# Two graph layers with residual norm: x kept on chip, turned blocks in the banks of row sums, a fourth bank for second products

## The chip, the cores and the metric

The kernel runs on one core of one Trainium2 chip. The metric is the device time of one execution in microseconds (us), lower is better. TensorE multiplies into PSUM, which has eight banks; VectorE, ScalarE and GpSimd work on SBUF and PSUM; SyncE (SP) issues the DMAs, all into one queue that sixteen DMA engines serve.

## The reference

```python
def reference(x, adj, u, weight, bias):          # x 8192x64, adj 8192x8192, f32
    keep = (u >= 0.1)
    h = layernorm(x + adj @ (x * keep / 0.9))
    return layernorm(h + adj @ (h @ weight) + bias)
```

adj is 256 MB of f32. Both layers multiply with all of it, and the second needs h, which needs the first.

## The kernel before

adj is cut into 16 x 16 tiles of 512 x 512, 1 MB each (four parts of 128 rows of the contraction). Tile (i, j) serves row i (output rows) and takes column block j. SBUF has 17 slots for tiles. `order_of_work` writes out a fixed list of jobs before the program is built, and `place_tiles` gives each tile a slot. TensorE works off the list in order. SP issues the loads in the same order, and each waits until the job that freed its slot is done (`tile_jobs_done`). The 256 tiles take 334 MB of loads: the list is made so that most tiles serve both layers with one load, and the rest come twice.

The kinds of jobs that matter here:
- `part`: row 0, in four parts. `part_turn` turns a part's block.
- `first` (L986): a tile's share of x's product, into the bank of row sums `sum_f[i % 2]`, of which it uses the left half.
- `second` (L1039), `pair` (L1033, two tiles), `both`, `early` (L1019), `chunk` and `rest` (L953, L954): products with h or with both operands. Each takes a bank out of `echo`, in turn, and VectorE adds it into its home in SBUF (L654 in the profile, called by `join`) and counts `added`. TensorE may not write a bank again before it was added.
- `raw` and `fused`: one tile for both layers with fewer multiplications; VectorE makes sums of the tile for them, and `combine` puts the products together at the end of the row.

When a row's sums are complete (`row_end`), VectorE copies them together with the shares from SBUF into `halves` (L841, L843), transposes them into the bank `turned` (L762), adds x (L776, eight instructions), and normalises (`normalise`, to L736). The result h is written to `stat`, beside the masked x that the first layer's matmuls use: `stat[:, block, 0:64]` holds masked x, `stat[:, block, 64:128]` is empty until h is there. Behind each row's end TensorE has a filler of some six halves of a job before it needs that h. x itself is loaded row by row into `x_res` (L486), two rows deep. At the start x and u come together in four loads `xu` into the last four slots, where VectorE makes masked x of them (L633).

The eight banks of PSUM: two for `products`, two for `sum_f`, one for `turned`, three for `echo`.

Of the kernel before, what the change touches and what calls it, by code (L numbers as in the profile page):

```python
# [27 lines left out]
ACT = mybir.ActivationFunctionType  # L28
# [19 lines left out]
FILL = 6  # L48
ECHO_BANKS = 3
WORK = {"chunk": 11, "rest": 11, "first": 11, "second": 11, "both": 22, "fused": 19, "pair": 22, "early": 44}  # L50
# [56 lines left out]
def turns(i):  # L107

    return i + PARTS
# [30 lines left out]
def order_of_work():  # L140
# [35 lines left out]
    for i in range(1, NB):  # L176
# [6 lines left out]
        while sum(HALVES[job[0]] for job in filler) < FILL:  # L183
            choice = [early] if lead < LEAD and early else [again] if i > 7 else []
            choice = [jobs_of for jobs_of in (*choice, light, again, early, heavy, near) if jobs_of]
            if pieces and (len(filler) == ECHO_BANKS if i > 1 else len(filler) % 2 == 0):
                filler += pieces.pop(0)
            else:
                filler.append(choice[0].pop(0))
            for job in filler[taken:]:  # L190
                put(job)
            taken = len(filler)
            if not turned:
                turned = True
                if i == 1:
                    jobs.append(("part_turn", PARTS - 1))
# [99 lines left out]

def resnorm_graph_layers(nc: bass.Bass, x, xu, adj_t, adj_parts, adj_0, adj_chunks, weight, bias, out):
    jobs = order_of_work()
# [37 lines left out]

    x_v = x.rearrange("(b p c) d -> p b (c d)", p=P, c=C)
    out_v = out.rearrange("(b p c) d -> p b (c d)", p=P, c=C)

    ctx = ExitStack()  # L340
    with ctx:
        def sb(name, shape):
            return ctx.enter_context(nc.sbuf_tensor(name, shape, F32))

        def sem(name):
# [9 lines left out]
        third = sb("third_partial", [P, B // 2])  # L355
        x_res = sb("x_res", [P, 2, C * D])
        halves = sb("halves", [P, B])
# [9 lines left out]

        h_bias = [x_res[:, :, :].rearrange("p n (c d) -> p (n c) d", d=D),
                  halves[:, :].rearrange("p (c d) -> p c d", d=D)]
        w2 = sb("w2", [P, 2 * D])  # L370
# [28 lines left out]
        def layer2_block(i):  # L399
# [5 lines left out]
            "p s (b n k d) -> p s b n k d", b=PARTS, n=2, d=D)  # L405

        psum = ctx.enter_context(nc.psum_tensor("psum", [P, 8, B], F32))
        banks = [psum[:, n] for n in range(8)]
        products = banks[0:2]
        sum_f = banks[2:4]  # L410
        turned = banks[4]
        echo = banks[5:8]
        scale_sum = echo[ECHO_BANKS - 1][:, 0:1]
# [20 lines left out]
        s_xu = [sem(f"xu_loaded_{n}") for n in range(XU)]  # L434
        s_res = [sem(f"x_res_loaded_{n}") for n in range(2)]
        s_small = sem("weight_bias_loaded")
        s_out = sem("out_stored")
        tile_jobs_done = sem("tile_jobs_done")
        dropped = sem("x_dropped")
        zeroed = sem("sums_zeroed")  # L440
        identity = sem("identity_ready")
# [29 lines left out]
        @block.sync  # L471
        def _(sp):
            for g in range(XU):
                sp.dma_start(tiles[:, staged + g], xu[g]).then_inc(s_xu[g], 16)
            rows_begun = 0
            for n, (tile, part, slot, freed, new, kind) in enumerate(loads):
                if n == len(loads) // 2:
                    for at in (0, D):
                        for beside in (0, D):
                            sp.dma_start(w2[at:at + D, beside:beside + D], weight).then_inc(s_small, 16)  # L480
                    sp.dma_start(bias_b[:, :], bias.rearrange("(a d) -> a d", a=1).to_broadcast([P, D])).then_inc(s_small, 16)
                if rows_begun == 0 and part == 1 or rows_begun >= 1 and kind in ("first", "fused") and tile[0] == rows_begun:
                    i = rows_begun
                    if i >= 2:
                        sp.wait_ge(turned_read, turns(i - 2))
                    sp.dma_start(x_res[:, i % 2], x_v[:, i]).then_inc(s_res[i % 2], 16)  # L486
                    rows_begun += 1
                if new and staged <= slot:
                    sp.wait_ge(dropped, XU)
                if freed:  # L490
                    sp.wait_ge(tile_jobs_done, freed)
                if part is not None:
                    to, source = tiles[:, slot, part], adj_parts[part, tile[1]]
                elif kind == "part":
                    to, source = tiles[:, slot], adj_0[tile[1], tile[2] - 1]
                elif kind == "chunk":
                    to, source = tiles[:, slot], adj_chunks[tile[1], tile[2]]
                else:
                    to, source = tiles[:, slot], adj_t[tile]
                sp.dma_start(to, source).then_inc(s_part[part] if part else s_arrived[slot], 16)  # L500
            for n, i in (*enumerate(finals[:-2]), (len(finals) - 1, finals[-1]), (len(finals) - 2, finals[-2])):
                if n == len(finals) - 1:
                    sp.wait_ge(last_y_ready, 1)
                else:
                    sp.wait_ge(y_ready, n + 1)
                sp.dma_start(out_v[:, i:i + 2], layer2[:, i // 2].rearrange("p (b k) -> p b k", b=2)).then_inc(s_out, 16)
            sp.wait_ge(s_out, 16 * len(finals))
# [31 lines left out]
        def _(act):  # L539
            norms = 0  # L540

            def norm(squares, centred_rows, root_ap, var_ap):
# [5 lines left out]
                act.activation(root_ap, var_ap, ACT.Sqrt).then_inc(rooted, 1)  # L548

            for job in jobs:  # L550
                if job[0] == "part_end":
# [23 lines left out]
        def _(dve):  # L575
# [54 lines left out]
            for g in range(XU):  # L630
                dve.wait_ge(s_xu[g], 16)
                t = slice(g * PARTS * C, (g + 1) * PARTS * C)
                dve.scalar_tensor_tensor(  # L633
                    out=stat[:, t, 0:D].rearrange("p (b k) d -> p b k d", b=PARTS), in0=xu_stage[:, g, :, 1], scalar=DROP,
                    in1=xu_stage[:, g, :, 0], op0=ALU.is_ge, op1=ALU.mult).then_inc(dropped, 1)
                dve.wait_ge(dropped, g + 1)
                dve.tensor_reduce(out=largest[:, g:g + 1], in_=stat[:, t, 0:D], axis=AX.XY,
                                  op=ALU.max).then_inc(dve_step, 1)
# [100 lines left out]
            def turn_part(q):  # L739

                rows = r[:, q:q + 1, :]
                t = turned[:, :].rearrange("p (c f) -> p c f", c=C)[:, q:q + 1]
                dve.wait_ge(s_res[0], 16)
                if q:
                    dve.wait_ge(h_ready, q)
                dve.wait_ge(turned_ready, q + 1)
                step(dve.scalar_tensor_tensor(out=rows, in0=t[:, :, 0:D], scalar=KEPT,
                                              in1=x_res[:, 0].rearrange("p (c d) -> p c d", c=C)[:, q:q + 1],
                                              op0=ALU.mult, op1=ALU.add))
# [5 lines left out]
            def turn(i):  # L755


                k = turns(i) - 1
                dve.wait_ge(s_res[i % 2], 16 * (i // 2 + 1))
                dve.wait_ge(h_ready, k)  # L760
                source = sum_f[i % 2] if i < EARLY else halves
                last = dve.transpose(turned[:, 0:B // 2], source[:, 0:B // 2])  # L762
                if i < EARLY:
                    last.then_inc(half_by_dve, 1)
                    dve.wait_ge(half_by_dve, turns(i))
                else:
                    step(last)
                t = turned[:, 0:B // 2].rearrange("p (c e f) -> p c e f", c=C, f=QUAD)
                x_rows = x_res[:, i % 2].rearrange("p (c d) -> p c d", c=C)
                for side in range(2):  # L770
# [104 lines left out]
        def _(pe):  # L875
# [29 lines left out]
            for at, job in enumerate(jobs):  # L905
                kind = job[0]
                if kind == "part":
                    _, q, g = job
                    bank = part_bank(q)
                    if g == 0 and q >= 2:  # L910
                        pe.wait_ge(half_by_act, q - 1)
                        pe.wait_ge(half_by_dve, q - 1)
                    if g == 0 and q:
# [20 lines left out]
                elif kind == "part_turn":  # L934
# [6 lines left out]
                    pe.wait_ge(half_by_dve, q + 1)  # L941
                    pe.transpose(turned[:, of_part(q)], halves[:, of_part(q)], ident[:, :]).then_inc(turned_ready, 1)
                elif kind in ("chunk", "rest"):
# [12 lines left out]
                elif kind in ("raw", "fused", "first", "both"):  # L956
# [21 lines left out]
                    elif kind != "fused":  # L978
                        if begun.get("f") != i:
                            if i <= 2:  # L980
                                pe.wait_ge(half_by_act, turns(i - 2))
                            pe.wait_ge(half_by_dve, turns(i - 2))
                        ends = jobs[at + 1] == ("row_end", i)
# [64 lines left out]
                elif kind == "final":  # L1048
# [3 lines left out]
                    if n_final >= 2:  # L1052
                        pe.wait_ge(product_read, n_final - 1)
                    else:
                        pe.wait_ge(half_by_dve, turns(NB - 1))
                        pe.wait_ge(combined, 2 * combined_rows(NB - 1))
# [45 lines left out]
```

## Time and profile before

| | |
|---|---|
| median of 3 runs | 898.15 us (898.11 to 898.16) |
| profiled execution | 898.45 us, span 896.5 us |
| TensorE busy | 863.1 us (96%), mean granted clock 0.995 |
| VectorE busy | 560.9 us (63%) |
| ScalarE, GpSimd busy | 21.3 us, 25.3 us |
| main DMA queue | 358.74 MB, 96.9% of sixteen engines' span |
| x loads | 16 of 128 KB |

Busy shares are means over the whole span. The time of an execution is somewhat longer than the span, which runs from the first to the last instruction. Matmuls come as two records each, and two of them run side by side, so the time of a group is read from its first start to the next group's start.

### The profile page before, as it was taken

How to read it: one execution, taken by the hardware profiler on the slowest of the kernel's cores; microseconds unless marked ns; L12 is line 12 of the kernel's file. 1: busy time of each engine (PE TensorE's matmuls, PEld its weight loads, DVE VectorE, ACT ScalarE, POOL GpSimd, SP SyncE). 2: the span in 40 equal slices, each digit the busy share in tenths (PEclk: the TensorE clock that was granted, in tenths of full speed). 3: DMA queues.
4: the chain of work that ended last, by engine and by line, in shares of the span. 5: the costliest groups of instructions: out<-in, count | busy, mean ns of one | idle time of the engine just before them, and what ended most of it. 6: DMA issues, size and time to landing. Idle time of an engine off the chain costs nothing.

```text
span 896.5 us, 15757 instructions
## 1 busy us (share of the span) xinstructions
PE 863.1 (96%) x6790; PEld 482.7 (54%) x6790; DVE 560.9 (63%) x1144; ACT 21.3 (2%) x59; POOL 25.3 (3%) x24
## 2 busy tenths in 40 slices
PE   3899999999999999999999999999999999999996
PEld 2664554445767546555555564646545566456432
DVE  6356123145155757775777777778777777867755
ACT  0100000000000000000000000000000000000011
POOL 3000000000000000000000000000000000000133
PEclk9999999999999999999999999999999999999998
DMA  9999999999999999999999999999999999999962
GB/s 373 412 416 420 421 419 420 421 420 421 420 420 420 419 421 419 421 400 402 420 421 406 423 419 397 419 372 422 372 410 421 415 423 419 420 423 419 420 256 71
DMA packets 55412, 359.73 MB, mean 401 GB/s; under 512 B 6448, under 2 KB 10544, under 8 KB 12592
## 3 DMA queue, kind: packets, MB, share of 16 engines
q1 hardware_dynamic: 55344, 358.74, 96.9%
q8 instruction: 54, 0.88, 0.4%
q14 instruction: 14, 0.11, 0.0%
HBM read 356.61 MB, written 2.10 MB: 400 GB/s over the span
## 4 chain that ended last, share of the span: by engine, by line
PE 85%; DMA 7%; DVE 4%; SPq 2%; issue 2%; ACT 0%; POOLq 0%; POOL 0%; DVEq 0%
PE psum L1033 20%; PE psum L986 19%; PE psum L967 8%; PE psum L1001 8%; PE psum L995 8%; PE psum L1019 6%; DMA tiles<-adj_chunks 5%; PE psum L953 5%; PE psum L974 4%; PE psum L1039 4%; DMA tiles<-adj_t 2%; PE psum L930 1%; SPq L500 1%; DVE layer L654 1%; DVE layer L709 1%
## 5 line engine op out<-in xcount | busy, mean ns | idle before, releaser
L986 PE MATMUL psum<-tiles,stat 128*64 128x256 f32 x1952 | 218.3, 379 | 1.6 <-DMA tiles<-adj_t 1.6
L1033 PE MATMUL psum<-tiles,stat 128*64 128x512 f32 x944 | 210.3, 593 | 0.6 <-issue 0.3
L654 DVE TENSOR_TENSOR layer<-psum,layer 128x512 f32<-128x512 f32 (+1 forms) x143 | 98.7, 690 | 154.6 <-PE psum L1033 58.0
L986 PEld LDWEIGHTS psum<-tiles,stat 128*64 128x64 f32 x1952 | 147.1, 137 | 72.4 <-issue 7.5
L1033 PEld LDWEIGHTS psum<-tiles,stat 128*64 128x64 f32 x944 | 69.2, 137 | 119.8 <-issue 115.8
L690 DVE TENSOR_TENSOR tiles<-tiles 128x512 f32<-128x512 f32 x90 | 62.2, 691 | 53.8 <-PE psum L976 52.2
L1003 PE MATMUL psum<-tiles,stat 128*64 128x256 f32 x360 | 92.6, 380 | 0.0
L969 PE MATMUL psum<-tiles,stat 128*64 128x256 f32 x360 | 92.4, 379 | 0.0
L967 PE MATMUL psum<-tiles,stat 128*64 128x256 f32 x360 | 92.4, 379 | 0.0
L967 PEld LDWEIGHTS psum<-tiles,stat 128*64 128x64 f32 x360 | 49.3, 137 | 37.8 <-issue 16.7
L678 DVE TENSOR_TENSOR tiles<-tiles 128x512 f32<-128x512 f32 x90 | 60.6, 684 | 8.0 <-DMA tiles<-adj_t 8.0
L693 DVE TENSOR_TENSOR tiles<-tiles 128x512 f32<-128x512 f32 x90 | 62.3, 692 | 3.1
L695 DVE TENSOR_TENSOR tiles<-tiles 128x512 f32<-128x512 f32 x90 | 61.6, 684 | 0.0
L1019 PE MATMUL psum<-tiles,stat 128*64 128x512 f32 x256 | 56.3, 593 | 2.9 <-issue 2.9
L930 PE MATMUL psum<-tiles,stat 128*64 128x128 f32 x512 | 34.1, 292 | 17.4 <-DMA tiles<-adj_parts 15.6
L969 PEld LDWEIGHTS psum<-tiles,stat 128*64 128x64 f32 x360 | 49.3, 137 | 0.0
L1001 PE MATMUL psum<-tiles,stat_homes 128*64 128x256 f32 x192 | 49.3, 379 | 0.0
L995 PE MATMUL psum<-tiles,stat_homes 128*64 128x256 f32 x192 | 49.3, 379 | 0.0
L997 PE MATMUL psum<-tiles,stat_homes 128*64 128x256 f32 x192 | 49.3, 379 | 0.0
L1003 PEld LDWEIGHTS psum<-tiles,stat 128*64 128x64 f32 x360 | 48.8, 137 | 0.0
L953 PE MATMUL psum<-tiles,stat 128*64 128x512 f32 x96 | 45.1, 600 | 0.9 <-DMA tiles<-adj_chunks 0.9
L954 PE MATMUL psum<-tiles,stat 128*64 128x512 f32 x96 | 45.1, 600 | 0.0
(100 smaller groups left out, 852.5 us busy)
## 6 DMA issues: line engine op xcount, KB each, us to landing
tiles<-adj_t SPq DMA_DIRECT2D x306, 1024.0 KB, 13.6
tiles<-adj SPq DMA_DIRECT2D x12, 1024.0 KB, 19.2
tiles<-adj_chunks SPq DMA_DIRECT2D x12, 1024.0 KB, 20.4
tiles<-xu SPq DMA_DIRECT2D x4, 1024.0 KB, 8.0
tiles<-adj_parts SPq DMA_DIRECT2D x16, 256.0 KB, 17.6
x_res<-x SPq DMA_DIRECT2D x16, 128.0 KB, 14.4
out<-layer SPq DMA_DIRECT2D x8, 256.0 KB, 2.2
w<-weight SPq DMA_DIRECT2D x4, 16.0 KB, 10.2
```

The source lines that it names most:

```text
L654: return dve.tensor_tensor(out=to, in0=addend, in1=to, op=ALU.add)
L690: dve.tensor_tensor(out=tile[:, top, left], in0=tile[:, top, left], in1=tile[:, top, right], op=ALU.add).then_inc(operands_ready, 1)
L693: dve.tensor_tensor(out=tile[:, bottom, left], in0=tile[:, bottom, left], in1=tile[:, top, left], op=ALU.add).then_inc(operands_ready, 1)
L953: pe.matmul(bank[0:D, :], stat[:, c, half], moving[:, n], start=True, stop=True)
L967: pe.matmul(products[0][low, left], stat[:, j * C + k, 0:D], tile[:, k, left], start=new and k == 0, stop=False, skip_group_check=True)
L969: pe.matmul(products[0][high, left], stat[:, j * C + 2 + k, 0:D], tile[:, 2 + k, left], start=new and k == 0, stop=False, skip_group_check ...
L986: last = pe.matmul(sum_f[i % 2][to, left], stat[:, j * C + c, 0:D], tile[:, c, columns], start=begun.get("f") != i and c == 0, stop=ends a ...
L995: pe.matmul(products[1][low, left], t[:, 2, k], tile[:, k, left], start=False, stop=False, skip_group_check=True)
L1001: pe.matmul(products[0][low, right], t[:, 1, k], tile[:, 2 + k, right], start=False, stop=False, skip_group_check=True)
L1003: last = pe.matmul(products[0][high, right], stat[:, j * C + 2 + k, D:2 * D], tile[:, 2 + k, left], start=False, stop=False, skip_group_ch ...
L1019: last = pe.matmul(bank[to, :], stat[:, j * C + c, half], tile[:, c], start=c == 0, stop=c == C - 1)
L1033: last = pe.matmul(bank[to, :], stat[:, j * C + c, D:2 * D], tile[:, c], start=c == 0, stop=c == C - 1)
```

## The change

- While `xu` lies in its slots, ScalarE copies x out of it into the half of `stat` where h will stand (`x_kept` counts the copies). VectorE reads x from there when it turns a row, and h is written over it afterwards. The loads into `x_res`, their semaphores and the DRAM argument `x` go. SP waits for `x_kept` before it loads into the slots of `xu`.
- `turned` has no bank of its own any more: a turned block goes to the right half of the bank of row sums that it comes from. TensorE therefore waits for `turned_read` (the turned block was read) where it waited for the copies of the sums.
- The bank that comes free is a fourth one for `echo`.
- In `order_of_work` the number of light jobs ahead of the pieces in a row's filler was `ECHO_BANKS`, 3; it is now a constant of its own, 2.
- `h_bias` at the end of the kernel uses two free blocks of `layer1`.

```diff
-ECHO_BANKS = 3
+ECHO_BANKS = 4
+JOINS_LAST = 2
...
-            if pieces and (len(filler) == ECHO_BANKS if i > 1 else len(filler) % 2 == 0):
+            if pieces and (len(filler) == JOINS_LAST if i > 1 else len(filler) % 2 == 0):
...
-        x_res = sb("x_res", [P, 2, C * D])
...
-        h_bias = [x_res[:, :, :].rearrange("p n (c d) -> p (n c) d", d=D),
-                  halves[:, :].rearrange("p (c d) -> p c d", d=D)]
+        h_bias = [layer1[:, n].rearrange("p (c d) -> p c d", d=D) for n in (1, 2)]
...
+        def rows_of_x(g, half):
+
+            return stat[:, g * PARTS * C:(g + 1) * PARTS * C, half].rearrange("p (b k) d -> p b k d", b=PARTS)
...
-        turned = banks[4]
-        echo = banks[5:8]
+        turned = [bank[:, B // 2:B] for bank in sum_f]
+        echo = banks[4:8]
...
-                if rows_begun == 0 and part == 1 or rows_begun >= 1 and kind in ("first", "fused") and tile[0] == rows_begun:
-                    i = rows_begun
-                    if i >= 2:
-                        sp.wait_ge(turned_read, turns(i - 2))
-                    sp.dma_start(x_res[:, i % 2], x_v[:, i]).then_inc(s_res[i % 2], 16)
-                    rows_begun += 1
                 if new and staged <= slot:
                     sp.wait_ge(dropped, XU)
+                    sp.wait_ge(x_kept, XU)
...
+            for g in range(XU):
+                act.wait_ge(s_xu[g], 16)
+                act.activation(rows_of_x(g, slice(D, 2 * D)), xu_stage[:, g, :, 0], ACT.Copy).then_inc(x_kept, 1)
...
-                dve.wait_ge(s_res[i % 2], 16 * (i // 2 + 1))
                 dve.wait_ge(h_ready, k)
                 source = sum_f[i % 2] if i < EARLY else halves
-                last = dve.transpose(turned[:, 0:B // 2], source[:, 0:B // 2])
+                last = dve.transpose(turned[i % 2], source[:, 0:B // 2])
...
-                t = turned[:, 0:B // 2].rearrange("p (c e f) -> p c e f", c=C, f=QUAD)
-                x_rows = x_res[:, i % 2].rearrange("p (c d) -> p c d", c=C)
+                t = turned[i % 2].rearrange("p (c e f) -> p c e f", c=C, f=QUAD)
+                x_rows = stat[:, i * C:(i + 1) * C, D:2 * D]
...
                     if g == 0 and q >= 2:
-                        pe.wait_ge(half_by_act, q - 1)
-                        pe.wait_ge(half_by_dve, q - 1)
+                        pe.wait_ge(turned_read, q - 1)
...
                         if begun.get("f") != i:
-                            if i <= 2:
-                                pe.wait_ge(half_by_act, turns(i - 2))
-                            pe.wait_ge(half_by_dve, turns(i - 2))
+                            pe.wait_ge(turned_read, turns(i - 2))
...
                     if n_final >= 2:
                         pe.wait_ge(product_read, n_final - 1)
                     else:
-                        pe.wait_ge(half_by_dve, turns(NB - 1))
+                        pe.wait_ge(turned_read, turns(NB - 1))
                         pe.wait_ge(combined, 2 * combined_rows(NB - 1))
```

How it moves instructions. SP's queue of DMAs, where rows 1 and 2 begin; before (L500 loads a tile, L486 a row of x):

```order
L500 DMA tiles<-adj_chunks 128x2048 [waits tile_jobs_done] x2
L486 DMA x_res<-x 128x256
L500 DMA tiles<-adj_t 128x2048 [waits tile_jobs_done] x8
L500 DMA tiles<-adj_chunks 128x2048 [waits tile_jobs_done]
L500 DMA tiles<-adj_t 128x2048 [waits tile_jobs_done] x3
L500 DMA tiles<-adj_chunks 128x2048 [waits tile_jobs_done]
L500 DMA tiles<-adj_t 128x2048 [waits tile_jobs_done] x7
L486 DMA x_res<-x 128x256 [waits turned_read]
L500 DMA tiles<-adj_t 128x2048 [waits tile_jobs_done] x3
L500 DMA tiles<-adj_chunks 128x2048 [waits tile_jobs_done]
```

and now (L496 loads a tile):

```order
L496 DMA tiles<-adj_chunks 128x2048 [waits tile_jobs_done] x2
L496 DMA tiles<-adj_t 128x2048 [waits tile_jobs_done] x8
L496 DMA tiles<-adj_chunks 128x2048 [waits tile_jobs_done]
L496 DMA tiles<-adj_t 128x2048 [waits tile_jobs_done] x3
L496 DMA tiles<-adj_chunks 128x2048 [waits tile_jobs_done]
L496 DMA tiles<-adj_t 128x2048 [waits tile_jobs_done] x9
L496 DMA tiles<-adj_chunks 128x2048 [waits tile_jobs_done]
```

The x loads are gone from between the tiles; the last tile of the chunks comes one load earlier or later.

TensorE towards the end of row 2, before (L1019 are heavy jobs, L986 light ones):

```order
L1019 MATMUL psum<-tiles,stat 64x512 [waits second_added]
L1019 MATMUL psum<-tiles,stat 64x512 x7
L986 MATMUL psum<-tiles,stat 64x256 [waits tile_arrived_1]
L986 MATMUL psum<-tiles,stat 64x256 x7
L986 MATMUL psum<-tiles,stat 64x256 [waits tile_arrived_6]
L986 MATMUL psum<-tiles,stat 64x256 x7
L986 MATMUL psum<-tiles,stat 64x256 [waits tile_arrived_13]
L986 MATMUL psum<-tiles,stat 64x256 x7
L986 MATMUL psum<-tiles,stat 64x256 [waits tile_arrived_14]
L986 MATMUL psum<-tiles,stat 64x256 x7
```

and now (L1014 heavy, L981 light):

```order
L981 MATMUL psum<-tiles,stat 64x256 [waits tile_arrived_11]
L981 MATMUL psum<-tiles,stat 64x256 x7
L981 MATMUL psum<-tiles,stat 64x256 [waits tile_arrived_1]
L981 MATMUL psum<-tiles,stat 64x256 x7
L1014 MATMUL psum<-tiles,stat 64x512 [waits second_added,tile_arrived_13,tile_arrived_6]
L1014 MATMUL psum<-tiles,stat 64x512 x7
L1014 MATMUL psum<-tiles,stat 64x512 [waits second_added]
L1014 MATMUL psum<-tiles,stat 64x512 x7
L981 MATMUL psum<-tiles,stat 64x256 [waits tile_arrived_14]
L981 MATMUL psum<-tiles,stat 64x256 x7
```

One heavy job with its two tiles has moved into row 2, between the light ones, from behind the row's end.

ScalarE at the start of the program, now:

```order
L548 ACT_TABLE_LOAD
L548 ACTIVATE stat<-tiles 128x16x64 [waits xu_loaded_0]
L548 ACTIVATE stat<-tiles 128x16x64 [waits xu_loaded_1]
L548 ACTIVATE stat<-tiles 128x16x64 [waits xu_loaded_2]
L548 ACTIVATE stat<-tiles 128x16x64 [waits xu_loaded_3]
L552 ACTIVATE halves<-psum 64x128 [waits tile_jobs_done]
```

The four copies stand between the load of the table and the copy of the first part's sums; before, nothing stood there.

## Rows read from the trace of the kernel before

**Rows 1.** The page, parts 1 and 3: busy time and share, DMA queue.
```profile
PE 863.1 (96%) x6790; PEld 482.7 (54%) x6790; DVE 560.9 (63%) x1144; ACT 21.3 (2%) x59; POOL 25.3 (3%) x24
...
q1 hardware_dynamic: 55344, 358.74, 96.9%
```

**Rows 2.** Stretches of 25 us: busy time per engine, clock, DMA share, GB/s.
```profile
300.00:325.00 25.00, 23.89 (x220) 15.16 (x218) 17.13 (x44) 0.62 (x2) 0.00 (x0) 1.00 1.02 420
...
425.00:450.00 25.00, 24.69 (x196) 14.06 (x194) 17.85 (x44) 0.62 (x2) 0.00 (x0) 1.00 1.02 422
...
575.00:600.00 25.00, 25.00 (x185) 13.07 (x183) 18.94 (x47) 0.62 (x2) 0.00 (x0) 1.00 0.92 377
```

**Rows 3.** The chain that ended last: start us, us, what.
```profile
142.16 1.73 PE psum L986 x16
143.88 3.43 PE psum L1033 x16
...
305.47 18.73 DMA tiles<-adj_t
...
442.12 0.31 issue
```

**Rows 4.** Timeline of TensorE at two stalls: start, us, what, idle before.
```profile
187.07 8.37 PE L1019 MATMUL psum<-tiles,stat 128*64 128x512 f32 x38 [1.89 <-issue]
...
324.25 1.95 PE L986 MATMUL psum<-tiles,stat 128*64 128x256 f32 x16 [0.54 <-DMA tiles<-adj_t]
```

**Rows 5.** Waits from 446 us to the end: us in total, times, longest.
```profile
PE psum L1039 <- DVE layer L654: 1.4, 1, 1.4
...
PE psum L1033 <- DVE layer L654: 0.3, 1, 0.3
```

**Rows 6.** DMA issues, page part 6: count, KB each, us to landing.
```profile
x_res<-x SPq DMA_DIRECT2D x16, 128.0 KB, 14.4
```

**Rows 7.** x loads issued to 305.5 and to 424.2; DMA from 22.9 to 24.2.
```profile
L486 SPq DMA_DIRECT2D x_res<-x x7: 431/506/2073, 6.8 to 291.6; - x7
...
L486 SPq DMA_DIRECT2D x_res<-x x9: 431/432/2073, 6.8 to 380.0; - x9
...
DMA packets 289, 0.50 MB, mean 386 GB/s; under 512 B 30, under 2 KB 58, under 8 KB 289
```

**Rows 8.** Timeline of TensorE and VectorE, end of row 14.
```profile
769.95 10.47 PE L1033 MATMUL psum<-tiles,stat 128*64 128x512 f32 x48
...
772.38 0.42 DVE L841 TENSOR_TENSOR halves<-psum,layer 64x256 f32<-64x256 f32 x1
...
779.47 0.48 DVE L736 SCALAR_TENSOR_TENSOR stat<-work,h_scale,rstd 128x256 f32<-128x256 f32 x1
...
780.96 2.29 DVE L654 TENSOR_TENSOR layer<-psum,layer 128x512 f32<-128x512 f32 x3
781.80 1.94 PE L1039 MATMUL psum<-tiles,stat 128*64 128x512 f32 x8 [1.37 <-DVE layer L654]
```

**Rows 9.** Timeline of TensorE, end of row 15.
```profile
837.09 10.47 PE L1033 MATMUL psum<-tiles,stat 128*64 128x512 f32 x48
847.82 3.65 PE L1033 MATMUL psum<-tiles,stat 128*64 128x512 f32 x16 [0.26 <-DVE layer L654]
```

**Rows 10.** A ScalarE group; timeline of VectorE and SP at the start.
```profile
L546 ACT ACTIVATE work<-layer 128x512 f32<-128x512 f32 x6 | 3.8, 630 | 27.7 <-DVE layer L851 27.7
...
13.17 1.22 DVE L633 SCALAR_TENSOR_TENSOR stat<-tiles 128x1024 f32<-128x1024 f32 x1
...
28.99 2.13 SPq L500 DMA_DIRECT2D tiles<-adj_chunks  x1
```

**Rows 11.** Instructions that read x_res, by line; groups of the transposition.
```profile
L776 DVE SCALAR_TENSOR_TENSOR work<-psum,x_res x120: 279/286/297, 132.2 to 843.0; 32x128 f32<-32x128 f32 x120
...
L762 DVE STREAM_TRANSPOSE psum<-halves 128x256 f32<-128x256 f32 x14 | 6.4, 460 | 0.5
...
L762 DVE STREAM_TRANSPOSE psum<-psum 128x256 f32<-128x256 f32 x1 | 0.5, 465 | 6.2 <-PE psum L986 6.2
```

More of the change, by code:

```diff
@@ L294, in place_tiles, with resnorm_graph_layers @@
     return loads, place
-def resnorm_graph_layers(nc: bass.Bass, x, xu, adj_t, adj_parts, adj_0, adj_chunks, weight, bias, out):
+def resnorm_graph_layers(nc: bass.Bass, xu, adj_t, adj_parts, adj_0, adj_chunks, weight, bias, out):
     jobs = order_of_work()
@@ L434, in resnorm_graph_layers @@
         s_xu = [sem(f"xu_loaded_{n}") for n in range(XU)]
-        s_res = [sem(f"x_res_loaded_{n}") for n in range(2)]
         s_small = sem("weight_bias_loaded")
@@ L439, in resnorm_graph_layers @@
         dropped = sem("x_dropped")
+        x_kept = sem("x_kept")
         zeroed = sem("sums_zeroed")
@@ L474, in _ @@
                 sp.dma_start(tiles[:, staged + g], xu[g]).then_inc(s_xu[g], 16)
-            rows_begun = 0
             for n, (tile, part, slot, freed, new, kind) in enumerate(loads):
@@ L633, in _ @@
                 dve.scalar_tensor_tensor(
-                    out=stat[:, t, 0:D].rearrange("p (b k) d -> p b k d", b=PARTS), in0=xu_stage[:, g, :, 1], scalar=DROP,
+                    out=rows_of_x(g, slice(0, D)), in0=xu_stage[:, g, :, 1], scalar=DROP,
                     in1=xu_stage[:, g, :, 0], op0=ALU.is_ge, op1=ALU.mult).then_inc(dropped, 1)
@@ L741, in turn_part @@
                 rows = r[:, q:q + 1, :]
-                t = turned[:, :].rearrange("p (c f) -> p c f", c=C)[:, q:q + 1]
-                dve.wait_ge(s_res[0], 16)
+                t = turned[part_bank(q)][:, 0:P].unsqueeze(1)
+                dve.wait_ge(x_kept, XU)
                 if q:
@@ L747, in turn_part @@
                 step(dve.scalar_tensor_tensor(out=rows, in0=t[:, :, 0:D], scalar=KEPT,
-                                              in1=x_res[:, 0].rearrange("p (c d) -> p c d", c=C)[:, q:q + 1],
+                                              in1=stat[:, q:q + 1, D:2 * D],
                                               op0=ALU.mult, op1=ALU.add))
@@ L941, in _ @@
                     pe.wait_ge(half_by_dve, q + 1)
-                    pe.transpose(turned[:, of_part(q)], halves[:, of_part(q)], ident[:, :]).then_inc(turned_ready, 1)
+                    pe.transpose(turned[part_bank(q)][:, 0:P], halves[:, of_part(q)], ident[:, :]).then_inc(turned_ready, 1)
                 elif kind in ("chunk", "rest"):
@@ L1086 @@
     arrays = {
-        "x": np.ascontiguousarray(x),
         "xu": np.ascontiguousarray(xu).reshape(XU, P, C, B),
```

1 line of the change is left out of this document (removed).

## The prediction

> **What bounds the kernel now.** I read the page first for the shares. TensorE is busy for 863.1 us of 896.5, and the DMA queue fills 96.9% of sixteen engines' span [rows 1]. Two resources near their limit are an average over stages, so the next view is the table of stretches. It splits the run. At 300 to 325 us the DMA moves 420 GB/s at a share of 1.02 while TensorE has gaps, 23.89 of 25 us; at 425 to 450 TensorE has almost none at 422 GB/s; at 575 to 600 TensorE is at 25.00 and the DMA has sagged to 377 GB/s [rows 2]. So tiles set the pace first and matmuls later. The chain of work that ended last shows the change-over. It goes through a DMA only three times, and the last is a 1 MB tile issued at 305.47 us that takes 18.73 us to land, at 324.20 [rows 3]. TensorE's own line shows who waited for it: a group of 16 matmuls, 1.73 us of work [rows 3], begins at 324.25 after 0.54 us of idle put down to the tile's DMA [rows 4]. What arrives earlier before that point makes the kernel shorter. What arrives earlier behind it is worth something only where TensorE still waits for it.
>
> Behind it the list of waits from 446 us to the end has two of note for the long matmuls, and both end with VectorE's L654: 1.4 us at L1039 and 0.3 us at L1033 [rows 5]. L654 adds a bank of second products into its home and so frees the bank; TensorE had used up its three.
>
> **The x loads.** The change takes away sixteen loads of 128 KB [rows 6]. Seven of them are issued before the deciding tile is [rows 7]. They stand ahead of it in the same queue, which is never empty there, so their time is what the tile comes earlier. At the full 420 GB/s, 131,072 B take 0.31 us. In a short stretch at 23 us, where one such load lands, the mean is 386 GB/s [rows 7]; that makes 0.34 us. Seven are 2.2 to 2.4 us, and I take 2.4. TensorE can use it: the stalls of 1.89 us at 187 and 0.54 us at 324 [rows 4] and those between them are there to be given back.
>
> The next thing that could hold TensorE is at 442.12, where the chain has 0.31 us of "issue" ahead of a group of L1033 [rows 3]; the profile names nobody. If it is a tile landing, that wait shrinks too, since nine x loads have gone by then [rows 7]: plus 0.3. If not: plus 0. I take 0.3, since the DMA still runs at 422 GB/s in that stretch [rows 2]. The DMA part is 2.7 us, between 2.2 and 2.9 (nine at 0.31 are 2.8). The seven loads of x behind it count for nothing.
>
> One page of the Trainium skill would price the loads higher. "DMA: Bandwidth & Descriptors", section Bandwidth, gives 0.95 us for 64 KB by itself and 6.15 us for 1 MB; by it the seven would be worth at least 6.7 us and the kernel would take some 889 us, an estimate. The trace speaks against it: in this queue 1 MB takes 2.5 us of the stream.
>
> **The fourth bank of second products.** Row 14 first. Three pairs, 48 records of L1033, begin at 769.95 [rows 8]. At 3.43 us for 16 [rows 3] they end at 780.25, but the next group, L1039, begins at 781.80. VectorE is late: it comes to the first half of the row sums (L841) at 772.38, then has to turn and normalise, and reaches the first L654 at 780.96 [rows 8]. With four banks L1039 need not wait for that addition. It still needs h of row 14, which L736 writes from 779.47 for 0.48 us, to 779.95 [rows 8]: 0.3 us before 780.25. The gain is 781.80 - 780.25 = 1.55 us. Next late could be the pair behind it, which takes the first bank again: it would begin at 780.25 + 1.72 = 781.97, and the first addition ends at 780.96 + 0.69 = 781.65. So nothing.
>
> Row 15 has the same picture. Three pairs from 837.09 end at 847.39, and the fourth begins at 847.82 [rows 9]: 0.43 us. Together 2.0 us. Bounds: 1.7 by the idle time [rows 5], 2.0 by the starts, and 0 from below, should L1039 have to wait for h after all. Both lie behind the last tile wait, so they come on top of the DMA part. Behind 851 us TensorE goes from pair to product without a stop of note, so the last additions and stores shift with it. In the first 130 us the bank waits exist too, but tiles set the pace there: 0.
>
> **What is added.** Four ScalarE copies of 128x1024. A 128x512 takes 0.63 us [rows 10], so at most 1.3 each and 5 in all. The fourth source is there before VectorE begins its fourth pass at 13.17 [rows 10]; the copies end by 15, while ScalarE has no other work. SP's new wait stands at the load that it issues at 28.99 [rows 10]: 14 us of cover. Without that cover the queue would run dry, and each microsecond would cost one. I put 0.
>
> Waits on the copies of a block become waits on its reading. For row i TensorE asks that row i-2 has been turned. Fifteen rows are turned between 132.2 and 843.0 [rows 11], 51 us apart on average, so that is long past: 0. L776 reads x from another tensor in the same shape, 0.29 us each: 0. The transposition inside one bank is there once already, at 465 ns against 460 from SBUF [rows 11]: 0.
>
> **The moved jobs.** In rows 2 and 3 the pairs of heavy jobs (L1019) come one or two light jobs earlier, and one of them ahead of row 2's end. The work and the tiles up to row 4 are the same. TensorE work that comes sooner only moves the stall of 1.89 us at 187, and the tile that lands at 324 has the same bytes before it. Behind row 2's end two heavy jobs still stand ahead of the first use of its h, more than the chain to h needs (7.6 us in row 14, from 772.38 to 779.95). 0.
>
> **Sum.** 2.7 + 2.0 = 4.7 us. The profiled execution took 898.45 us for a span of 896.5 and so would take 893.75; it stands 0.3 above the median of 898.15, and from that: 893.4.
>
> **Rivals.**
> Only the banks help. The x loads are hidden if TensorE can't move up, for instance if VectorE holds it at 324 as well. The profile puts that wait down to the DMA alone. 898.15 - 2.0 = 896.2.
> Only the loads help. L1039 in row 14 needs h, with 0.3 us of cover; a bank wait may also only move one group on. 898.15 - 2.7 = 895.4.
> Nothing comes of either, 898.15: it would take a queue that is not the limit before 324, against 420 GB/s at a share of 1.02.
> Small loads cost more than their bytes. At twice the share of the stream, 0.68 us, the time is 898.15 - 7 x 0.68 - 0.3 - 2.0 = 891.1. The 386 GB/s speak against it. The skill's page above would have it so.
> The other side: the turned block in a bank of row sums makes VectorE's chain of each row longer. It touches that bank with the transposition and eight L776, 0.47 + 2.52 = 3.0 us a row. Cover is 0.3 us in row 14 and in a plain row 10.3 us of filler (three groups of 3.43) less 7.6, that is 2.7. If these nine took twice as long, row 14 would lose 2.7 us, six other rows behind 446 us 0.3 each, and row 14's gain of 1.55 would be gone: 898.15 - 2.7 - 0.4 + 2.7 + 1.8 = 899.6. It gets slower than before from about 2.8 us more a row. Against it: meanwhile the matmuls of the next row write the other of the two banks.
>
> **Chances.** Forecast 0.70, with a range of its own of 892.3 to 894.6; only the loads 0.11; only the banks 0.06; nothing 0.04; dearer loads 0.05; slower 0.04. The range for 8 in 10 holds the forecast and the loads-only case: 892.0 to 895.9. A change of 0.2%, 1.8 us, is about what a measurement can tell from none. Under 896.35 lie the forecast, the loads-only case, the dearer loads and most of banks-only: faster 0.90, same 0.06, slower 0.04.
>
> **What the profile after would show.** No x load among the DMA issues. The deciding tile landing near 321.8, and no matmul behind it that waits for a DMA. L1039 of row 14 straight behind its three pairs, and no wait on L654 in row 15. ScalarE's copies over by 15 us. Wrong would be: a wait ended by a tile behind 330 us, a longer L776, L1039 waiting for h, or SP held at 29 us.

## The result and the profile after

The changed kernel takes 892.86 us, median of 4 runs (892.74 to 893.27), against 898.15 us (898.11 to 898.23): a ratio of 0.9941, 95% interval 0.9929 to 0.9954. That is 5.29 us less; the forecast was 4.7 less. The profiled execution took 893.27 us for a span of 891.5 us, where before it took 898.45 us for 896.5: 5.0 us less in the span.

The page of the kernel after, parts 1 and 3, in the columns of [rows 1]:

```profile
PE 861.4 (97%) x6790; PEld 489.3 (55%) x6790; DVE 560.9 (63%) x1144; ACT 25.6 (3%) x63; POOL 25.3 (3%) x24
...
q1 hardware_dynamic: 53040, 356.64, 96.8%
```

TensorE runs the same 6790 matmuls, ScalarE four instructions more. The queue moves 358.74 - 356.64 = 2.10 MB less, the sixteen loads of 128 KB; the group of [rows 6] is gone from the DMA issues. The shares tell nothing else, so the next view is the same three stretches as in [rows 2]:

```profile
300.00:325.00 25.00, 24.04 (x217) 15.00 (x214) 16.03 (x42) 0.62 (x2) 0.00 (x0) 1.00 1.01 419
425.00:450.00 25.00, 25.00 (x188) 13.26 (x186) 18.05 (x45) 0.62 (x2) 0.00 (x0) 1.00 1.01 421
575.00:600.00 25.00, 25.00 (x172) 12.06 (x168) 17.34 (x44) 0.62 (x2) 0.00 (x0) 1.00 0.92 369
```

At 300 to 325 TensorE still has gaps and the DMA still runs at 419 GB/s: tiles still set the pace there. At 425 to 450 the 0.31 us that TensorE lacked before are back. The chain of work that ended last shows the change-over (first fence), and the timeline of TensorE shows who waited (second; start us, us, what, idle before in brackets):

```profile
303.50 18.36 DMA tiles<-adj_t
321.90 1.95 PE psum L981 x16
```

```profile
321.90 1.95 PE L981 MATMUL psum<-tiles,stat 128*64 128x256 f32 x16 [0.54 <-DMA tiles<-adj_t]
...
436.17 7.04 PE L1028 MATMUL psum<-tiles,stat 128*64 128x512 f32 x32
443.03 3.62 PE L981 MATMUL psum<-tiles,stat 128*64 128x256 f32 x32
446.49 1.89 PE L1034 MATMUL psum<-tiles,stat 128*64 128x512 f32 x8
```

The deciding tile lands at 303.50 + 18.36 = 321.86 us, before at 324.20 [rows 3]: 2.34 us sooner, and the same 0.54 us of idle stands ahead of its matmuls. It is the last DMA in the chain. At the place of the "issue" at 442.12 [rows 3] the 32 matmuls of L1028 (L1033 before) now stand in one piece. The same place in the kernel before:

```profile
438.51 3.60 PE L1033 MATMUL psum<-tiles,stat 128*64 128x512 f32 x16
442.42 3.65 PE L1033 MATMUL psum<-tiles,stat 128*64 128x512 f32 x16 [0.31 <-issue]
445.88 3.75 PE L986 MATMUL psum<-tiles,stat 128*64 128x256 f32 x32
449.46 1.89 PE L1039 MATMUL psum<-tiles,stat 128*64 128x512 f32 x8
```

From 438.51 to 449.46 it took 10.95 us, and after, from 436.17 to 446.49, 10.32 us for the same work: 0.63 us went, twice the printed 0.31. 0.48 of it lies at the gap itself (442.42 - 438.51 = 3.91 us from start to start, 3.43 without a gap [rows 3]), 0.15 in the 48 matmuls behind it. Most of that 0.15 is a second wait, which the rows of the matmuls do not print. The rows of the weight loads do, and they name the DMA; before and after:

```profile
447.68 1.49 PEld L986 LDWEIGHTS psum<-tiles,stat 128*64 128x64 f32 x16 [0.33 <-DMA tiles<-adj_t]
```

```profile
443.04 3.17 PEld L981 LDWEIGHTS psum<-tiles,stat 128*64 128x64 f32 x30 [0.28 <-issue]
```

So the last tile that TensorE waited for before was not that of 324. It is one that is issued at 430.09 and lands 17.6 us later, at 447.7, behind ten x loads; after, it lands at 444.3 and nothing waits for it.

The end of row 14 on TensorE and VectorE answers to [rows 8], the end of row 15 to [rows 9]:

```profile
766.95 10.47 PE L1028 MATMUL psum<-tiles,stat 128*64 128x512 f32 x48
777.25 1.89 PE L1034 MATMUL psum<-tiles,stat 128*64 128x512 f32 x8
```

```profile
776.46 0.48 DVE L735 SCALAR_TENSOR_TENSOR stat<-work,h_scale,rstd 128x256 f32<-128x256 f32 x1
...
777.95 2.28 DVE L653 TENSOR_TENSOR layer<-psum,layer 128x512 f32<-128x512 f32 x3
```

```profile
832.50 13.90 PE L1028 MATMUL psum<-tiles,stat 128*64 128x512 f32 x64
```

L1034 (before L1039) begins at 777.25, 10.30 us after the three pairs, as forecast, and before the first addition of L653 (before L654) at 777.95. h was there at 776.46 + 0.48 = 776.94, so the cover was 0.31 us. In row 15 four pairs stand in one piece of 64. The waits of TensorE from 446 us to the end, in the columns of [rows 5], hold neither of the two that stood there:

```profile
PE psum L1059 <- DVE layer L653: 0.3, 1, 0.3
```

(This one is a wait at a line of the last products. It stands there in every kernel of this study.) ScalarE's fourth copy, and the reading of the turned block (L774, before L776) with its transposition (L760, before L762), whose rows of before are in [rows 10, 11]:

```profile
13.39 1.06 ACT L548 ACTIVATE stat<-tiles 128x1024 f32<-128x1024 f32 x1 [1.44 <-DMA tiles<-xu]
```

```profile
L774 DVE SCALAR_TENSOR_TENSOR work<-psum,stat x120: 277/286/299, 133.3 to 838.4; 32x128 f32<-32x128 f32 x120
...
L760 DVE STREAM_TRANSPOSE psum<-halves 128x256 f32<-128x256 f32 x14 | 6.4, 460 | 0.5
```

The copies are over at 14.45 us, 9 us before SP comes to the first load that waits for them, the same load that it issued at 28.99 before [rows 10]:

```profile
23.55 7.96 SPq L496 DMA_DIRECT2D tiles<-adj_chunks  x1
```

Neither of the two that now work in a bank of row sums got longer: a median of 286 ns and a mean of 460 ns, as before.

So the time came from two places. By the starts of the same jobs, TensorE is ahead by 324.25 - 321.90 = 2.35 us at the deciding tile, by 449.46 - 446.49 = 2.97 at 446 us, and in row 14 by 781.80 - 777.25 = 4.55. Row 15 adds its share (847.82 less the start of the fourth pair, 832.50 + 10.30 = 842.80, is 5.02), and at that the spans' 5.0 us are full.

One more thing belongs to these numbers. The profiled execution after is the longest of its four, and its stream of tiles began late. The first instruction of VectorE, which waits for the first `xu` load, before and after:

```profile
5.72 1.23 DVE L633 SCALAR_TENSOR_TENSOR stat<-tiles 128x1024 f32<-128x1024 f32 x1 [5.72 <-DMA tiles<-xu]
```

```profile
5.96 1.22 DVE L632 SCALAR_TENSOR_TENSOR stat<-tiles 128x1024 f32<-128x1024 f32 x1 [5.96 <-DMA tiles<-xu]
```

It is 0.24 us behind from the start. So the 2.34 us at the deciding tile are 2.6 us by this count, and the experiments below bear the larger number out.

### The profile page after: what moved, and what is told of

It is laid out like the page before. It is cut to its first block, busy times and chain, and to the rows that moved or that the text cites. A ratio compares the mean times of both kernels' runs of the same rounds, so it can differ in the third digit from the quotient of the medians.

```text
span 891.5 us, 15749 instructions
## 1 busy us (share of the span) xinstructions
PE 861.4 (97%) x6790; PEld 489.3 (55%) x6790; DVE 560.9 (63%) x1144; ACT 25.6 (3%) x63; POOL 25.3 (3%) x24
## 3 DMA queue, kind: packets, MB, share of 16 engines
q1 hardware_dynamic: 53040, 356.64, 96.8%
## 4 chain that ended last, share of the span: by engine, by line
PE 90%; DMA 7%; SPq 1%; issue 1%; DVE 1%; POOLq 0%; POOL 0%; ACT 0%; DVEq 0%
PE psum L1028 22%; PE psum L981 20%; PE psum L964 8%; PE psum L996 8%; PE psum L990 8%; PE psum L1014 6%; PE psum L950 4%; PE psum L971 4%; DMA tiles<-adj_t 4%; PE psum L1034 4%; DMA tiles<-adj_chunks 3%; PE psum L927 1%; SPq L496 1%; DVE layer L653 0%; PE psum L1059 0%
## 5 line engine op out<-in xcount | busy, mean ns | idle before, releaser
L981 PE MATMUL psum<-tiles,stat 128*64 128x256 f32 x1952 | 217.9, 379 | 1.5 <-DMA tiles<-adj_t 1.5
L1028 PE MATMUL psum<-tiles,stat 128*64 128x512 f32 x944 | 209.8, 593 | 0.0
L653 DVE TENSOR_TENSOR layer<-psum,layer 128x512 f32<-128x512 f32 (+1 forms) x143 | 98.7, 690 | 146.9 <-PE psum L1028 55.2
L981 PEld LDWEIGHTS psum<-tiles,stat 128*64 128x64 f32 x1952 | 152.7, 137 | 66.0 <-issue 7.4
L1028 PEld LDWEIGHTS psum<-tiles,stat 128*64 128x64 f32 x944 | 68.5, 137 | 119.4 <-issue 115.4
L964 PEld LDWEIGHTS psum<-tiles,stat 128*64 128x64 f32 x360 | 49.3, 137 | 38.4 <-issue 17.0
L1014 PE MATMUL psum<-tiles,stat 128*64 128x512 f32 x256 | 58.1, 607 | 2.2 <-issue 2.2
L966 PEld LDWEIGHTS psum<-tiles,stat 128*64 128x64 f32 x360 | 49.3, 137 | 0.0
L998 PEld LDWEIGHTS psum<-tiles,stat 128*64 128x64 f32 x360 | 48.8, 137 | 0.0
L927 PEld LDWEIGHTS psum<-tiles,stat 128*64 128x64 f32 x512 | 31.7, 149 | 22.3 <-issue 18.1
L950 PE MATMUL psum<-tiles,stat 128*64 128x512 f32 x96 | 43.0, 593 | 0.5 <-DMA tiles<-adj_chunks 0.5
```

What stands on the lines that cost most here:

```text
L653: return dve.tensor_tensor(out=to, in0=addend, in1=to, op=ALU.add)
L927: last = pe.matmul(sum_f[bank][to, 0:P], stat[:, j * C + c, 0:D], moving[:, c], start=j == 0 and c < 2, stop=j == NB - 1 and c >= 2, skip_ ...
L950: pe.matmul(bank[0:D, :], stat[:, c, half], moving[:, n], start=True, stop=True)
L964: pe.matmul(products[0][low, left], stat[:, j * C + k, 0:D], tile[:, k, left], start=new and k == 0, stop=False, skip_group_check=True)
L966: pe.matmul(products[0][high, left], stat[:, j * C + 2 + k, 0:D], tile[:, 2 + k, left], start=new and k == 0, stop=False, skip_group_check ...
L981: last = pe.matmul(sum_f[i % 2][to, left], stat[:, j * C + c, 0:D], tile[:, c, columns], start=begun.get("f") != i and c == 0, stop=ends a ...
```

## The experiments

Three groups: what each half does alone, what each of the forecast's zeros is worth, and where the load's price and its border in time are.

**The loads alone.** The kernel before with x kept, no x loads, but three banks of second products and a bank of its own for the turned block:

```diff
 ECHO_BANKS = 3
+JOINS_LAST = 3
...
-        x_res = sb("x_res", [P, 2, C * D])
...
         turned = banks[4]
...
+            for g in range(XU):
+                act.wait_ge(s_xu[g], 16)
+                act.activation(rows_of_x(g, slice(D, 2 * D)), xu_stage[:, g, :, 0], ACT.Copy).then_inc(x_kept, 1)
...
```

> x kept on chip and no x loads; turned in its own bank, three banks for second products, order of work as before. Theory (tiles ahead of 324 us): 7 x 0.34 us earlier there and the 0.54 us lost at 442 gone, so 2.9 us under the kernel before, 895.3. Row 14's and row 15's waits on L653 should still stand (1.4 and 0.3 us idle). Rival (the loads are hidden and the banks did all): 898.1.

Measured: 895.01 us (894.88 to 895.18), before 898.26; ratio 0.9963, interval 0.9951 to 0.9976. The last DMA of its chain, and its waits from 446 us on:

```profile
304.37 17.32 DMA tiles<-adj_t
```

```profile
PE psum L1037 <- DVE layer L653: 1.4, 1, 1.4
PE psum L1031 <- DVE layer L653: 0.3, 1, 0.3
```

The tile lands at 321.69, and both bank waits of [rows 5] are still there, with the same times. So the loads are worth 898.26 - 895.01 = 3.25 us by the medians and 896.5 - 893.4 = 3.1 by the spans.

**The banks alone.** The kernel before with the turned block in the bank of row sums and four banks of second products; the x loads and the order stay:

```diff
-ECHO_BANKS = 3
+ECHO_BANKS = 4
...
-            if pieces and (len(filler) == ECHO_BANKS if i > 1 else len(filler) % 2 == 0):
+            if pieces and (len(filler) == 3 if i > 1 else len(filler) % 2 == 0):
...
-        turned = banks[4]
-        echo = banks[5:8]
+        turned = [bank[:, B // 2:B] for bank in sum_f]
+        echo = banks[4:8]
...
```

> The kernel before with the turned blocks in the banks of row sums and four banks for second products; x still loaded, order as before. Theory: only the waits of rows 14 and 15 go, 1.55 + 0.45 = 2.0 us, 896.1; the stalls on tiles at 322 to 326 and at 442 us stay where they were. Rival (the fourth bank lets TensorE run ahead everywhere): below 895. Rival (a turned block in the bank of row sums slows VectorE's chain): 898 or more, with L776's counterpart over 0.29 us.

Measured: 896.03 us (895.65 to 896.57), before 898.26; ratio 0.9975, interval 0.9965 to 0.9985. Its deciding tile, and TensorE in row 14:

```profile
305.48 18.57 DMA tiles<-adj_t
```

```profile
769.49 10.47 PE L1030 MATMUL psum<-tiles,stat 128*64 128x512 f32 x48
779.79 1.89 PE L1036 MATMUL psum<-tiles,stat 128*64 128x512 f32 x8
```

The tile lands at 324.05, as before, and L1036 follows its three pairs after 10.30 us. The banks are worth 2.23 us. The halves add up, 3.25 + 2.23 = 5.5, against 5.29 for both, within what the medians scatter.

**The order alone.** The kernel before with the join of rows 2 and 3 placed behind two filler jobs, as the change has it:

```diff
-            if pieces and (len(filler) == ECHO_BANKS if i > 1 else len(filler) % 2 == 0):
+            if pieces and (len(filler) == 2 if i > 1 else len(filler) % 2 == 0):
```

> The kernel before, only the constant in the order of work changed from 3 to 2 (heavy jobs of rows 2 and 3 one or two light jobs earlier). Theory: the tile before 324 us has the same bytes ahead of it, so 898.15 within 0.3 us; the stall at 187 us gets smaller and moves. Rival (the order gave part of the 5.3 us): 897 or less.

Measured: 898.25 us (897.83 to 898.55), ratio 0.9998, interval 0.9989 to 1.0007. And the changed kernel with the old order, `JOINS_LAST = 3`:

> The changed kernel with that constant back at 3. Theory: as the changed kernel, 892.9 within 0.3 us. Rival (the new order is needed with four banks): 893.5 or more.

Measured: 892.97 us (892.94 to 893.08), ratio 0.9941, interval 0.9928 to 0.9953. The order is worth nothing in either kernel.

**The fourth bank taken out again.** The changed kernel with three banks, the turned block still in the bank of row sums and one bank unused:

```diff
-ECHO_BANKS = 4
+ECHO_BANKS = 3
...
-        echo = banks[4:8]
+        echo = banks[4:7]
```

> The changed kernel with three banks for second products, one bank of PSUM unused, turned blocks still in the banks of row sums. Theory: 892.86 + 2.0 = 894.9, and the same as the kernel that has x kept but turned in a bank of its own, since sharing a bank costs nothing. Rival (sharing costs VectorE time): above that kernel by 0.5 us or more.

Measured: 895.11 us (894.82 to 895.33), before 898.17; ratio 0.9965, interval 0.9953 to 0.9978; the waits of 1.4 and 0.3 us are back. It is 3.06 us under its before, the kernel with the loads alone 3.25: two kernels that differ in where the turned block stands and in the order, and that take the same time. So sharing the bank costs nothing that can be measured.

**Only the two waits.** The changed kernel, with four banks, where two jobs of rows 14 and 15 wait as if there were three:

```diff
                     if n_second >= ECHO_BANKS:
-                        pe.wait_ge(added, n_second - ECHO_BANKS + 1)
+                        ahead = 3 if job in (("second", 11, 14), ("pair", 8, 14)) else ECHO_BANKS
+                        pe.wait_ge(added, n_second - ahead + 1)
```

> The changed kernel with four banks, but at two jobs alone, the ones that waited in rows 14 and 15, TensorE waits as if there were three. Theory: all that the fourth bank gave lies in these two, so 892.86 + 1.55 + 0.45 = 894.9. Rival (it gave something elsewhere): less than 894.3.

Measured: 895.09 us (895.02 to 895.19), ratio 0.9966, interval 0.9953 to 0.9978. TensorE in row 14:

```profile
766.84 10.47 PE L1029 MATMUL psum<-tiles,stat 128*64 128x512 f32 x48
778.66 1.94 PE L1035 MATMUL psum<-tiles,stat 128*64 128x512 f32 x8 [1.36 <-DVE layer L653]
```

778.66 - 766.84 = 11.82 us where the changed kernel has 10.30: 1.52 us in row 14. Two waits bring back the whole of the bank part (895.09 less the 893.02 of the kernel with loads behind 380 us, below, is 2.07), and the time is that of the kernel with three banks throughout, 895.11. So the fourth bank does nothing anywhere else that can be measured.

**Loads ahead of 324 us.** The changed kernel, with the x loads of rows 0 to 6 issued where they stood into a tensor that nothing reads:

```diff
+                if rows_begun == 0 and part == 1 or rows_begun >= 1 and kind in ("first", "fused") and tile[0] == rows_begun:
+                    i = rows_begun
+                    if i in range(0, 7):
...
+                        sp.dma_start(x_res[:, i % 2], x_v[:, i]).then_inc(s_res[i % 2], 16)
```

> The changed kernel with the x loads of rows 0 to 6 back in their places in the queue; nobody reads what they bring. Theory: the tile before 324 us comes 7 x 0.34 = 2.4 us later, so 892.86 + 2.4 = 895.2. Rival (the gain came from the copy on chip or from SP's fewer waits, not from the queue): 892.9.

Measured: 895.59 us (895.54 to 895.84), before 898.12; ratio 0.9972, interval 0.9961 to 0.9982. The tile and TensorE behind it:

```profile
305.50 18.61 DMA tiles<-adj_t
```

```profile
324.15 1.95 PE L996 MATMUL psum<-tiles,stat 128*64 128x256 f32 x16 [0.52 <-DMA tiles<-adj_t]
```

Seven loads bring the stall back from 321.90 to 324.15, 2.25 us, and the time back by 2.57 (against 893.02, below). The two differ because of the late start of the profiled execution after: this one has its first `xu` load at 5.70 us, not at 5.96, and with that the 2.25 become 2.51.

Every kernel of this study has a trace, so the landing of this tile can be compared without leaning on one execution. It lands at 324.20, 324.38, 324.05 and 324.11 us in the four with the seven loads ahead of it (the kernel before, the order alone, the banks alone, this one), 324.19 on average. In the eight without them it lands at 321.86 (the kernel after) and otherwise between 321.37 and 321.74, 321.60 on average. That makes 2.58 us, or 0.37 us a load.

**Loads behind 380 us.** The same with rows 9 to 15, `if i in range(9, 16)`:

> The changed kernel with the x loads of rows 9 to 15 back, unread. Theory: they stand behind the last tile that TensorE waits for, so 892.9 within 0.3. The nearest tile behind it is ready 0.6 us before its use at 445, and the first of these loads stands behind it or just ahead of it, which could cost up to 0.1. Rival (every byte counts, since the queue is busy 97% of the span): 892.86 + 7 x 0.34 = 895.2.

Measured: 893.02 us (892.86 to 893.09), ratio 0.9943, interval 0.9929 to 0.9956. Seven loads of the same size cost nothing here that can be measured: what a load is worth depends on its place.

**The two loads between.** The same with rows 7 and 8, which lie between the deciding tile and 442 us:

> The changed kernel with the x loads of rows 7 and 8 back, unread; they stand behind the tile of 324 us and ahead of the tile of 442. In the changed kernel that tile is ready 0.43 us before its use. Theory: 2 x 0.34 - 0.43 = 0.25 us later, 893.1. Rival (free like all behind 324): 892.9. Rival (each counts in full): 893.5.

Measured: 893.33 us (893.16 to 893.53), before 898.17; ratio 0.9945, interval 0.9931 to 0.9959. TensorE at the place in question:

```profile
435.74 3.60 PE L1043 MATMUL psum<-tiles,stat 128*64 128x512 f32 x16
439.74 3.65 PE L1043 MATMUL psum<-tiles,stat 128*64 128x512 f32 x16 [0.40 <-issue]
443.20 3.65 PE L996 MATMUL psum<-tiles,stat 128*64 128x256 f32 x32
```

The gap is back, 4.00 us from start to start in place of 3.43, by nothing but two loads ahead of it in the queue. The profile calls it "issue", but it is a tile that lands late. The tile ahead of it in SP's queue, and the time to its landing:

```profile
421.27 0.33 SPq L508 DMA_DIRECT2D tiles<-adj_t  x1
DMA to landing us min/median/max: 18.4/18.4/18.4
```

It lands at 439.7, and the matmuls behind the gap begin at 439.74. In the kernel before the same tile is issued at 424.05 and lands 18.3 us later, at 442.3, and the matmuls begin at 442.42. In the kernel with loads behind 380 us it lands at 438.6, about 0.5 us before it is needed. 893.33 against 893.02 and 893.03 of kernels without these two loads is 0.3 us, near the scatter; the rows of the trace are the firmer sign.

**Every load twice.** The kernel before, each of the sixteen loads issued a second time into an unread tensor:

```diff
...
                     sp.dma_start(x_res[:, i % 2], x_v[:, i]).then_inc(s_res[i % 2], 16)
+                    if i >= 2:
+                        sp.wait_ge(s_dup[i % 2], 16 * (i // 2))
+                    sp.dma_start(x_dup[:, i % 2], x_v[:, i]).then_inc(s_dup[i % 2], 16)
```

> The kernel before with every x load made twice, the second one unread. Theory: seven more ahead of 324 us give 2.4 us, and at 442 us nine more give 3.1, of which the later one decides: 898.15 + 2.4 to 3.1, 900.6 to 901.3. Rival (a load costs little beside the tiles): 898.5 or less. Rival (small loads cost more than their bytes): over 902.

Measured: 901.95 us (901.76 to 902.41), before 898.12; ratio 1.0043, interval 1.003 to 1.0055: 3.83 us more, over what I expected. The last DMA of the chain, and TensorE around it:

```profile
432.79 18.59 DMA tiles<-adj_t
```

```profile
445.79 3.65 PE L1040 MATMUL psum<-tiles,stat 128*64 128x512 f32 x16 [0.97 <-issue]
449.24 1.93 PE L993 MATMUL psum<-tiles,stat 128*64 128x256 f32 x16
451.43 1.95 PE L993 MATMUL psum<-tiles,stat 128*64 128x256 f32 x16 [0.26 <-DMA tiles<-adj_t]
```

The last DMA of the chain is no longer the tile of 324 but one that lands at 451.38, with ten doubled loads ahead of it in the queue. It is the tile that the weight loads waited for at 447.68 in the kernel before, so it was already the last that counted there, and all ten loads count: 451.4 - 447.7 = 3.7 us by the landings, 3.83 by the medians, 0.37 to 0.38 us each. Two things were off in what I expected: I had counted nine loads, at 0.34.

**Seven loads twice.** To split those two, the same kernel with only rows 0 to 6 doubled:

```diff
+                    if i < 7:
...
```

> The kernel before, with the x loads of rows 0 to 6 issued twice and those of rows 7 to 15 once. With all sixteen twice the tile that lands at 451 decided, ten doubled loads behind. Theory: here only seven doubled loads stand ahead of both places, at 0.34 to 0.38 us each, so 898.15 + 2.4 to 2.7 = 900.5 to 900.8 us, and TensorE has no wait of 1.0 us near 445. Rival: the extra over my count came from the doubled loads before 324 alone (each dearer than I took it), and those of rows 7 to 9 did nothing: 901.9 again.

Measured: 900.89 us (900.66 to 901.47), before 898.21; ratio 1.0029, interval 1.0017 to 1.004. The last DMA of its chain and the places at 324 and 442:

```profile
307.89 18.92 DMA tiles<-adj_t
```

```profile
326.85 1.95 PE L994 MATMUL psum<-tiles,stat 128*64 128x256 f32 x16 [0.79 <-DMA tiles<-adj_t]
...
441.12 7.39 PE L1041 MATMUL psum<-tiles,stat 128*64 128x512 f32 x32
```

```profile
450.12 1.49 PEld L994 LDWEIGHTS psum<-tiles,stat 128*64 128x64 f32 x16 [0.35 <-DMA tiles<-adj_t]
```

2.68 us more, 0.38 a load. The chain names the tile of 324 again, which lands at 326.81, 2.6 us later than on average in the kernels with single loads. No idle is printed near 442, but the 32 matmuls take 7.39 us where the kernel after has 7.04, and the weight loads still wait for the later tile: the two small waits of the kernel before are still there. The three loads of rows 7 to 9 made the other 3.83 - 2.68 = 1.15 us, 0.38 each. So the loads between the two tiles count as well, through the later one.

A load added costs the same as a load taken away gives: 0.38 us against 0.37. The 2.34 / 7 = 0.33 of the one pair of traces is low because the profiled execution after began late.

**The copies three times.** The changed kernel, each ScalarE copy of x made three times in a row, with SP and VectorE waiting for all of them:

```diff
-                    sp.wait_ge(x_kept, XU)
+                    sp.wait_ge(x_kept, 3 * XU)
...
-                act.activation(rows_of_x(g, slice(D, 2 * D)), xu_stage[:, g, :, 0], ACT.Copy).then_inc(x_kept, 1)
+                for k in range(3):
+                    act.activation(rows_of_x(g, slice(D, 2 * D)), xu_stage[:, g, :, 0], ACT.Copy).then_inc(x_kept, 1)
+                    act.wait_ge(x_kept, 3 * g + k + 1)
...
```

> The changed kernel with each of ScalarE's four copies of x made three times, one after the other, so that the last ends at about 22 us in place of 14. Theory: SP needs them at 29 us, so nothing, 892.9. Rival (the copies lie on the path at the start): 5 us and more later.

Measured: 893.03 us (892.97 to 893.06), ratio 0.9942, interval 0.993 to 0.9955. ScalarE, and the load behind SP's wait:

```profile
5.71 13.03 ACT L549 ACTIVATE stat<-tiles 128x1024 f32<-128x1024 f32 x12 [3.69 <-DMA tiles<-xu]
```

```profile
23.95 7.33 SPq L496 DMA_DIRECT2D tiles<-adj_chunks  x1
```

Twelve copies end at 18.74 us, 4.3 us later than four, and still 5 us ahead of the load. Nothing moves.

## Why the prediction was right, point by point

**What bounds the kernel.** Right in the main, and shown: loads behind 380 us cost nothing, loads ahead of the tile at 324 cost their share of the queue, and the halves add up. Where the tiles stop setting the pace was put too early. After the tile of 324 TensorE waited for two more, those that land at 442.3 and 447.7; of the first I guessed, and the second I did not see. They were worth 0.6 us.

**The seven loads, 2.4 us.** The mechanism is right and the price a little low. In the one pair of traces they gave 2.34 by the landing and 2.35 by TensorE's start; over twelve traces, 2.58 us, 0.37 each and not 0.34. The landing was forecast near 321.8 and came at 321.86, and that close a hit is luck: the other seven kernels without the loads have it 0.1 to 0.5 us earlier. The price was taken from the 386 GB/s of one stretch of 1.3 us with one such load in it [rows 7].

**The wait at 442, 0.3 us.** The step that it is a tile was a guess, and the experiment with two loads shows it right. Its size was wrong: I took the printed 0.31 us, but the stretch around it is 0.63 us shorter now, 0.48 at this wait and most of the rest at the one for the next tile but one, at 447.68. These 0.3 us and the 0.2 of the seven loads are the difference between the forecast 2.7 and the measured 3.1 to 3.25 us of the DMA part.

**The fourth bank, 2.0 us.** 2.07 by the two waits put back, 2.23 by the banks alone. Row 14 was forecast at 1.55 and gave 1.55 (11.85 us from start to start before, 10.30 now), 1.52 by the two waits; h came 0.31 us ahead of the three pairs' end, against 0.3 forecast.

**The zeros.** The copies (1.06 us each, at most 1.3 forecast), SP's wait, L774 from another tensor, the transposition inside the bank and the order were all worth nothing; for the copies, the order and the bank each has a run of its own. One cover came out smaller: SP issues the load with the wait at 23.55 in the kernel after, not at 28.99, so the cover was 9 us and not 14. The waits on reading have no run of their own; no wait of TensorE in the profile after names them.

**The stalls early.** In the kernel after, TensorE has no gap at the place of the 1.89 us at 187 [rows 4], and waits elsewhere ahead of 324. I had said only that such stalls are there to be given back; what became of each of them makes no difference, since the tile at 324 gathers them all.

**The rivals.** Only the banks (896.2) and only the loads (895.4) turned out to be the times of the halves, 896.03 and 895.01. A slower chain in the shared bank is excluded by 895.11 against 895.01. Small loads are somewhat dearer than their bytes, 0.37 to 0.38 us against 0.31, but not the 0.68 of that rival. That nothing comes of either is excluded by the result.

The Trainium skill, "DMA: Bandwidth & Descriptors", section Bandwidth, gives 0.95 us for a transfer of 64 KB. Seven loads at no less than that would have been 6.7 us, an estimate; the traces disagree with 2.34 to 2.58 us. The page's figures are for DMAs issued from GpSimd, and here SyncE issues them.

## What to carry to other kernels

Find the last transfer that the engine waited for, and count what stands ahead of it in its queue: here only those loads were worth time, and nearly in full. The chain that ended last names a candidate, not always the last one: in the kernel before, two later tiles were waited for, and only a row of the weight loads named the DMA for the last. Before a price per transfer is read from one pair of traces, compare where their streams begin. A wait that the profile puts down to "issue" in a stretch where the queue is full may be a tile that lands late, and the starts of the groups around it tell its cost better than the idle time printed beside it.

## What the runs showed of the hardware

A 128 KB load in a queue that is never empty costs 0.37 to 0.38 us, whether it is taken away (seven: 2.58 us by the mean landings of twelve traces) or added (seven: 2.68 us by the medians; ten: 3.83), where its bytes at 420 GB/s make 0.31. VectorE's reads and its transposition in a PSUM bank whose other half holds row sums took 286 and 460 ns, the same as with a bank of their own.
